# Count blocks of one node per step instead of a pair, in a four-layer graph network

## The chip, the cores and the metric

The kernel runs on one core of one Trainium2 chip, as one launch. The metric is device time in microseconds of a whole execution; less is better. Engines are named as in the profile: PE (TensorE), PEld (its weight load), DVE (VectorE), ACT (ScalarE), POOL (GpSimd), SP (SyncE).

## The reference

6250 nodes have 64 features, and 206250 edges (`src`, `dst`) are sorted by `dst`. Four residual layers follow each other, each followed by a layer norm:

```python
x = _layernorm(x + _L0_gnn_ref(x, edge_attr_32, src, dst, ...))   # mlp: segment_sum(relu([x[src], x[dst], a] @ W1 + b1) @ W2 + b2, dst)
x = _layernorm(x + _L1_gnn_ref(x, edge_index, edge_attr_16, ...)) # gatv2: 4 heads, softmax over each node's edges, batch norm, gelu
x = _layernorm(x + _L2_gnn_ref(x, edge_index, W, a))              # gat: 1 head, softmax over each node's edges, elu
x = _layernorm(x + _L3_gnn_ref(x, src, dst))                      # mean of x[src] over each node's edges
```

The last layer's mean is `segment_sum(x[src], dst) / max(count, 1)`. All inputs are fp32.

## The kernel before

The edges lie in 1612 tiles of 128. Seven tiles make a batch (`B`), and there are 231 batches (`NB`). `prepare` makes tables from the lists of edges. Then `edge_pass` runs three times, as mlp, gatv2 and gat, with `dense` behind each for the work by node, and `mean_layer` comes last. In a trace the tiles of the passes begin with `mlp_`, `gatv_` and `gat_`.

**A batch of an edge pass.** POOL issues one indirect gather of table rows per tile (L469) into a ring of eight batches (`G`, `GQ = 8`). In mlp it waits for `z_made` of six batches back. SP loads the edges' window-relative destination numbers (`rel`), windows of the destination table (`win`) and edge features (`attrT`). DVE compares `rel` to make two one-hot arrays of 7 x 128 columns, `hot` (L487) and `same` (L494, ring of four). PE makes `z` from features and windows (`make_z`, L806 and L810), DVE adds the gathered rows (L508), ACT applies the nonlinearity, PE sums edges that share a destination (`make_sums`, L846), and ACT and SP write them out. mlp has the flag `hist`, under which DVE makes two more one-hots (`count`, L560 and L562) and PE counts the nodes as sources (`add_counts`, L855). Each engine has a `step(i)` in which the order of its work for batch i and its neighbours is written out by hand. `over_batches` runs the first `start` batches unrolled, and the rest in a hardware loop of `U` batches per round.

**Count blocks.** The mean layer gathers nothing. For each step, which is one edge tile together with one destination, there is a column of counts that says how many edges come from every source node. A source is split into a low part (128 values, `src_lo`) and a high part (49 values, `HI`), so a block of a step is a one-hot of 128 times a one-hot of keys. Before, a step holds a pair of nodes: 98 keys (`KEYS`), 4736 steps (`NS`) in 37 columns (`SB`). The steps are found in mlp's unrolled batches. `prepare` spreads tile numbers; SP stores the list `step_of` at batch 7 (L392, one number per element) and loads it back with the tiles' rows (`load_steps`); in batches 14 to 45 PE runs `turn_steps` (L881 to L886) for 37 groups of 128 steps, two a batch, with three copies by ACT each (`copy_cols`, L764); DVE mixes the keys (`step_work`). Then the blocks are built beside the passes: DVE makes one-hots of the next steps (`build_hots`, L635 and L637), PE multiplies them, one matmul of 98 columns per step into a PSUM bank, contiguous (`build_block`, L865), ACT copies groups of five blocks (`copy_block`, L729), and SP stores them to `blocks` in DRAM, once a batch. `BUILD` says which batches build how many: mlp nine a batch from 48, gatv2 five and gat ten a batch from 0, all to 215. Constants that DVE compares with (`iota_of`, `lane_of`, `rel_of`) lie in PSUM (`in_psum`) in bf16.

**The mean layer.** It runs over 74 half blocks of 64 steps (`MEAN_HALVES`). SP loads one (L1965), PE multiplies it by the nodes' features, split into three bf16 parts of 65 columns, with 49 matmuls of 195 columns (L2035), in which the weights are columns of the block with a stride. DVE adds the three parts, PE joins rows of one node (L2010, L2014), and the rest is division, the layer norm, and an indirect load and store by node.

## Time and profile before

| what | value |
|---|---|
| median of three runs | 8260.32 us (8241.33 to 8264.79) |
| span of the profiled execution | 6975.1 us |
| busy in it: PE, PEld, DVE, ACT, POOL | 80%, 70%, 68%, 21%, 71% |
| gathers of mlp, gatv2 and gat | 1612 each |
| iterations of the mean layer | 74 |

The span is the stretch that the profiler shows between the first and the last instruction; the measured time is longer. The stages follow each other with little overlap: `prepare` to 87 us, mlp to 2111, its dense to 2240, gatv2 to 4258, its dense to 4448, gat to about 6496, its dense to about 6600 and the mean layer to the end. PE's clock in the tables is a share of full speed: 1.00 is 2.4 GHz, 0.50 is 1.2 GHz, and values between are mixtures.

### The profile page before, as it was taken

The numbers are of one execution on the slowest core, as the hardware profiler recorded it, in microseconds if no ns is written. First come the engines' busy times: TensorE is split into PE (matmuls) and PEld (weight loads), VectorE is DVE, ScalarE is ACT, GpSimd is POOL, SyncE is SP. The second block draws the span as 40 slices with busy tenths as digits, with TensorE's granted clock in tenths as the row PEclk, the third lists the DMA queues.
The fourth block names the chain that finished last, engine by engine and source line by source line (L and its number), as shares of the span: only waits on it lengthen the run. The fifth ranks groups of instructions, "written<-read, shape, count | busy, mean of one in ns | idle before, by whom it ended". The sixth has DMA issues, their size and how long they took to land. (4 is left out here: it accounts for less than half of the span.)

```text
span 6975.1 us, 134144 instructions
## 1 busy us (share of the span) xinstructions
PE 5545.7 (80%) x36891; PEld 4916.1 (70%) x36891; DVE 4763.3 (68%) x7973; ACT 1449.0 (21%) x4328; POOL 4949.6 (71%) x5209
## 2 busy tenths in 40 slices
PE   5897888777776778888778885588888888888399
PEld 4676777666665666666666663588888888887399
DVE  4557777777755788888888875566666666666455
ACT  1112222222212222222222221222222222222200
POOL 4777777777775777777777776377777777777444
PEclk6556555666665555555555555555555555555599
DMA  6756666666653555555555553554545555554397
GB/s 158 180 144 155 159 159 159 159 158 160 159 149 87 152 146 146 146 145 146 145 146 145 146 146 80 63 112 110 110 110 110 110 110 110 110 110 95 117 360 292
DMA packets 1384856, 995.18 MB, mean 143 GB/s; under 512 B 927331, under 2 KB 1293029, under 8 KB 1375046
## 3 DMA queue, kind: packets, MB, share of 16 engines
q1 hardware_dynamic: 906390, 750.00, 36.6%
q0 software_dynamic: 165856, 169.99, 14.7%
q10 hardware_dynamic: 312400, 72.71, 5.1%
q8 instruction: 92, 1.51, 0.1%
q14 instruction: 118, 0.97, 0.0%
HBM read 676.85 MB, written 315.92 MB: 142 GB/s over the span
## 5 line engine op out<-in xcount | busy, mean ns | idle before, releaser
L469 POOL DMA_INDIRECT gat_G<-gat_src,src_cols x1612 | 1530.2, 949 | 592.8 <-issue 490.3
L469 POOL DMA_INDIRECT mlp_G<-mlp_src,src_cols x1612 | 1533.4, 951 | 533.5 <-issue 487.2
L469 POOL DMA_INDIRECT gatv_G<-gatv_src,src_cols x1612 | 1527.5, 948 | 524.8 <-issue 491.0
L810 PE MATMUL gat_z<-gat_win,gat_hot 128*128 128x1 f32 x3234 | 721.0, 352 | 274.4 <-DVE gat_msg L552 212.9
L810 PEld LDWEIGHTS gat_z<-gat_win,gat_hot 128*128 128x128 f32 x3234 | 707.3, 330 | 318.8 <-issue 279.7
L806 PE MATMUL gatv_z<-attr_w,gatv_attrT 112*128 112x448 f32 x462 | 425.1, 1024 | 408.6 <-DVE gatv_msg L552 398.8
L846 PE MATMUL gat_sums<-gat_msg,gat_same 128*128 128x65 f32 x3234 | 713.6, 410 | 0.0
L846 PEld LDWEIGHTS gat_sums<-gat_msg,gat_same 128*128 128x128 f32 x3234 | 708.2, 330 | 0.0
L846 PE MATMUL gatv_sums<-gatv_msg,gatv_same 128*128 128x68 f32 x3234 | 689.6, 403 | 0.0
L846 PEld LDWEIGHTS gatv_sums<-gatv_msg,gatv_same 128*128 128x128 f32 x3234 | 687.3, 321 | 0.1
L846 PE MATMUL mlp_sums<-mlp_act_out,mlp_same 128*128 128x64 f32 x3234 | 632.7, 374 | 0.0
L846 PEld LDWEIGHTS mlp_sums<-mlp_act_out,mlp_same 128*128 128x128 f32 x3234 | 604.6, 286 | 0.4 <-issue 0.4
L508 DVE TENSOR_TENSOR mlp_zs<-mlp_z,mlp_G 128x448 f32<-128x448 f32 x231 | 144.2, 624 | 642.0 <-DMA mlp_G<-mlp_src,src_cols 612.1
L806 PE MATMUL mlp_z<-attr_w,mlp_attrT 128*128 128x256 f32 (+1 forms) x924 | 482.6, 624 | 79.7 <-DVE mlp_hot L487 47.3
L508 DVE TENSOR_TENSOR gat_z<-gat_z,gat_G 128x7 f32<-128x7 f32 x231 | 40.1, 174 | 637.0 <-DMA gat_G<-gat_src,src_cols 636.8
L810 PEld LDWEIGHTS gatv_z<-gatv_win,gatv_hot 128*128 128x128 bf16 x4851 | 303.7, 134 | 232.3 <-issue 232.3
L806 PEld LDWEIGHTS gatv_z<-attr_w,gatv_attrT 112*128 112x128 f32 x462 | 115.7, 311 | 452.6 <-issue 451.9
L712 ACT ACTIVATE mlp_act_out<-mlp_zs 128x448 f32<-128x448 f32 x231 | 133.2, 577 | 1374.5 <-DVE mlp_zs L508 1283.5
L810 PEld LDWEIGHTS mlp_z<-mlp_win,mlp_hot 128*128 128x128 bf16 x4851 | 335.0, 132 | 115.3 <-issue 91.8
L865 PE MATMUL mlp_build_ps<-mlp_build_area 128*128 128x98 bf16 x1512 | 168.6, 260 | 300.3 <-ACT mlp_build_area L729 300.3
L508 DVE TENSOR_TENSOR gatv_z<-gatv_z,gatv_G 128x448 f32<-128x448 f32 x231 | 146.1, 632 | 365.6 <-DMA gatv_G<-gatv_src,src_cols 365.6
L865 PEld LDWEIGHTS mlp_build_ps<-mlp_build_area 128*128 128x128 bf16 x1512 | 103.3, 121 | 355.8 <-ACT mlp_build_area L729 312.3
(494 smaller groups left out, 10679.4 us busy)
## 6 DMA issues: line engine op xcount, KB each, us to landing
mean_block<-blocks SPq DMA_DIRECT2D x74, 1568.0 KB, 10.1
sums_gatv<-gatv_out_rows SPq DMA_DIRECT2D x231, 252.0 KB
sums_gat<-gat_out_rows SPq DMA_DIRECT2D x231, 231.0 KB, 2.4
blocks<-gat_build_area SPq DMA_DIRECT2D x216, 245.0 KB
mlp_rel<-rel_rows SPq DMA_DIRECT2D x231, 224.0 KB
sums_mlp<-mlp_out_rows SPq DMA_DIRECT2D x231, 224.0 KB
gatv_rel<-rel_rows SPq DMA_DIRECT2D x231, 224.0 KB
gat_rel<-rel_rows SPq DMA_DIRECT2D x231, 224.0 KB
```

The source lines that it names most:

```text
L469: pool.indirect_dma_start(out=G[:, b.gq, j * L.gathered:(j + 1) * L.gathered], out_offset=None, in_=L.gather_table, in_offset=bass.Indirec ...
L508: nc.vector.tensor_tensor(total.rearrange("p (b w) -> p b w", w=w), made.rearrange("p (b w) -> p b w", w=w), Gv[:, b.gq, :, L.gathered - w ...
L712: act.activation(act_out[:, b.q, :], zs[:, b.q, :], ACT.Relu).then_inc(act_done, 1)
L806: pe.matmul(z[b.q % 2][:, t0 * w:(t0 + nt) * w], attrT[0:nt * ax, b.q, g, :], S["attr_w"][ax][0:nt * ax, 0:nt * w], start=True, stop=True)
L810: last = pe.matmul(z[b.q % 2][:, j * w:(j + 1) * w], hot[:, b.q, j, :], win[:, b.q, j, part * w:(part + 1) * w], start=not ax and part == ...
L846: last = pe.matmul(sums[b.q % 2][:, j * L.msg:(j + 1) * L.msg], same[:, b.q, j, :], rhs, start=True, stop=True)
L865: last = pe.matmul(build_in[g % len(build_in)][:, j * KEYS:(j + 1) * KEYS], hot_src[:, b.c % 2, k + j, :], hot_key[:, b.c % 2, k + j, :], ...
```

## The change

A step holds one node. There are 7936 steps in 62 columns, with 49 keys each. Eight steps make an octet, which is the unit in which DVE, PE and ACT work, with two PSUM rings replaced by one bank that ACT has to empty before the next octet. mlp builds four octets a batch in batches 48 to 199, gatv2 two a batch in 8 to 199, gat none. ACT copies an octet into a half (128 steps, 1.6 MB) in SBUF, in the space of `masks` or `work`, and SP stores a half when it is full. In the one-hots of blocks and counts two steps lie innermost, so that every operand of the comparison has two packed bf16 elements there; `hot` of mlp and gatv2 is compared with a pattern of 32 packed lanes. PE therefore reads those one-hots with a stride of two elements, and writes a step's block to every eighth element of PSUM. Two-slot `same` in mlp, an `act_out` that shares the place of `zs` in mlp, and other sharing of memory make room. The steps are found in five portions at batches 8 to 55, with four groups a batch; the key mixing has two operations per portion instead of four; `U` is 16, and `start` is 24 in gatv2. The mean layer runs 62 iterations of 128 steps over contiguous weights, with five slots for blocks, and its setup of rows has fewer operations. The dense stages read the longer `step_of`. The diff, cut to its core:

```diff
-U = 8
+U = 16
...
-PAIRS = N // 2
-NS = ETILES + PAIRS - 1
-SB = NS // P
-assert SB * P == NS and NS // P + 1 <= 2 * D
-KEYS = 2 * HI
-STEP_ROWS = 40 * P
-NONE = 200.0
-GROUP = 5
+SB = -(-(ETILES + N - 1) // P)
+NS = SB * P
+STEP_ROWS = 64 * P
+assert SB <= D and NS <= STEP_ROWS and N + NTP <= STEP_ROWS
+FAR_KEY = 64.0
 PASS_C = 216
-BUILD = {"mlp": (48, PASS_C, 9, 0), "gatv2": (0, PASS_C, 5, 1512), "gat": (0, PASS_C, 10, 2592)}
-NSP = 2592 + PASS_C * 10
+K2, OCTET = 2, 8
+HALF_OCTETS = P // OCTET
+HALF_W = HI * P
+BUILD = {"mlp": (48, 200, 4, 0), "gatv2": (8, 200, 2, 608), "gat": (0, 0, 0, 992)}
 assert all(BUILD[a][3] + (BUILD[a][1] - BUILD[a][0]) * BUILD[a][2] == BUILD[b][3]
-           for a, b in (("mlp", "gatv2"), ("gatv2", "gat"))) and NSP >= NS
+           for a, b in (("mlp", "gatv2"), ("gatv2", "gat"))) and BUILD["gat"][3] * OCTET == NS
 ROW_W = 4 * P
-THIRD = -(-SB // 3)
-THIRDS = [(0, THIRD), (THIRD, THIRD - 1), (2 * THIRD - 1, THIRD - 1)]
-assert THIRDS[-1][0] + THIRDS[-1][1] == SB
-LOAD_AT, HOT_AT, GROUPS_AT, KEYS_AT = (8, 22, 34), (11, 25, 37), (14, 27, 39), (22, 34, 46)
-LOADS = 4
+PORTION = -(-SB // 5)
+PORTIONS = [(0, PORTION), (PORTION, PORTION)] + [(2 * PORTION + k * (PORTION - 1), PORTION - 1) for k in range(3)]
+assert PORTIONS[-1][0] + PORTIONS[-1][1] == SB
+LOAD_AT, HOT_AT, GROUPS_AT, KEYS_AT = (tuple(a + 8 * h for h in range(5)) for a in (8, 10, 11, 15))
+LOADS, GROUPS_EACH = 7, 4
...
-        same = sb("same", [P, Q, B, P])
+        SQ = Q if soft else 2
+        same = sb("same", [P, SQ, B, P])
         out_rows = sb("out_rows", [P, Q, B * L.row])
...
+        rel_of, lane_of, lanes_of = (consts[:, o:o + w] for o, w in ((0, NT), (LANES, 1), (LANES, D // 2)))
+        steps2_of = consts[:, STEPS2:CONSTS].rearrange("p (e k) -> p e k", k=K2)
...
-            hot_hi = sb("hot_hi", [P, 2, B, HI], BF16)
-            hot_lo = sb("hot_lo", [P, 2, B, P], BF16)
+            hot_hi = sb("hot_hi", [P, 2, OCTET // K2, HI, K2], BF16)
+            hot_lo = sb("hot_lo", [P, 2, OCTET // K2, P, K2], BF16)
...
+        build_from, build_end, per_batch, first_octet = BUILD[L.name]
+        block_count = (build_end - build_from) * per_batch
+        build_ps = pb("build_ps", [P, 512])
+        build_of = build_ps[:, 0:OCTET * HI].rearrange("p (h e) -> p h e", e=OCTET)
+        if per_batch:
+            ring = 2 * per_batch
+            hots = sb("hots", [P, max(ring * OCTET * (P + HI), PORTION * ROW_W if hist else 0)], BF16)
+            hot_src = hots[:, 0:ring * OCTET * P].rearrange("p (q g e k) -> p q g e k", q=ring, g=OCTET // K2, k=K2)
+            hot_key = hots[:, ring * OCTET * P:ring * OCTET * (P + HI)].rearrange(
+                "p (q g e k) -> p q g e k", q=ring, g=OCTET // K2, k=K2)
+            area = hots[:, :].bitcast(F32)
+        else:
+            area = sb("area", [P, TA])
+        if hist:
+            step_rows = hots[:, 0:PORTION * ROW_W].rearrange("p (b w) -> p b w", w=ROW_W)
...
-                o = i + (-2)
+                o = i + (-3)
                 if o.exists() and builds(o):
-                    wait(sp, blocks_copied, built(o))
-                    sp.dma_start(S["blocks"][:, bass.ds(first_of(o) * KEYS, per_batch * KEYS)],
-                                 block_out[:, o.c % 2, :]).then_inc(blocks_out[o.c % 2], 16)
+                    k, loops = half_of(o, per_batch)
+                    if k % HALF_OCTETS == 0:
+                        h = k // HALF_OCTETS - 1
+                        wait(sp, blocks_copied, octet(o, per_batch))
+                        sp.dma_start(S["blocks"][:, bass.ds((loops + (h + first_octet // HALF_OCTETS)) * HALF_W, HALF_W)],
+                                     halves[h % 2].rearrange("p h e -> p (h e)")).then_inc(blocks_out[h % 2], 16)
                 if hist and isinstance(i.n, int) and i.n == 1:
                     sp.wait_ge(S["steps_spread"], 16 * RB)
                     sp.dma_start(step_in[:, :], S["step_tile"][0:NS, :].rearrange("(b e) o -> b (e o)", e=P)
...
-                nc.vector.tensor_tensor(hot[:, b.q, :, :], relv[:, b.q, :, :],
-                                        bc(lane_of, 2, [P, B, P]), ALU.is_equal).then_inc(hot_made, 1)
+                if L.win_dt == BF16:
+                    nc.vector.tensor_tensor(
+                        hot[:, b.q, :, :].rearrange("p b (a e) -> p (b a) e", e=D // 2),
+                        rel[:, b.q, :].rearrange("p (b e) -> p b e", e=D // 2), bc(lanes_of, 1, [P, 4 * B, D // 2]),
+                        ALU.is_equal
+                    ).then_inc(hot_made, 1)
+                else:
+                    nc.vector.tensor_tensor(hot[:, b.q, :, :], relv[:, b.q, :, :],
+                                            bc(lane_of, 2, [P, B, P]), ALU.is_equal).then_inc(hot_made, 1)
 
...
-                wait(dve, sums_made, b.used(Q))
-                nc.vector.tensor_tensor(same[:, b.q, :, :], relv[:, b.q, :, :],
+                wait(dve, sums_made, b.used(SQ))
+                nc.vector.tensor_tensor(same[:, b.c % SQ, :, :], relv[:, b.q, :, :],
...
-            def build_hots(b):
-                wait(dve, blocks_made, built(b, back=2))
-                cols = bass.ds(first_of(b), per_batch)
-                nc.vector.tensor_tensor(hot_src[:, b.c % 2, :, :], bc(iota_of, 1, [P, per_batch, P]),
-                                        bc(S["src_lo"][:, cols], 2, [P, per_batch, P]), ALU.is_equal)
-                nc.vector.tensor_tensor(hot_key[:, b.c % 2, :, :], bc(iota_of[:, 0:KEYS], 1, [P, per_batch, KEYS]),
-                                        bc(S["keys"][:, cols], 2, [P, per_batch, KEYS]), ALU.is_equal
-                                        ).then_inc(hots_made, 1)
+            def build_hots(b, k):
+                if hist and isinstance(b.n, int) and b.n == build_from:
+                    dve.wait_ge(groups_made, SB)
+                wait(dve, blocks_made, octet(b, k + 1 - ring))
+                cols = bass.ds((octet(b, k) + first_octet) * OCTET, OCTET)
+                for hot_of, of_step, w in ((hot_src, S["src_lo"], P), (hot_key, S["keys"], HI)):
+                    last = nc.vector.tensor_tensor(
+                        hot_of[:, slot(b, k), :, :, :], bc(steps2_of[:, 0:w, :], 1, [P, OCTET // K2, w, K2]),
+                        bc(of_step[:, cols].rearrange("p (g k) -> p g k", k=K2), 2, [P, OCTET // K2, w, K2]), ALU.is_equal)
+                last.then_inc(hots_made, 1)
...
-                        chain(v.tensor_scalar(rho_h, rho_h, -1.0, 2.0, ALU.max, ALU.min))
-                        chain(v.scalar_tensor_tensor(out=mixed_h, in0=rho_h, scalar=1.0, in1=rho_h,
-                                                     op0=ALU.subtract, op1=ALU.mult))
-                    if n == KEYS_AT[h] + 1:
-                        chain(v.scalar_tensor_tensor(out=mixed_h, in0=mixed_h, scalar=2.0, in1=rho_h,
-                                                     op0=ALU.mult, op1=ALU.add))
-                        chain(v.scalar_tensor_tensor(out=keys_h, in0=mixed_h, scalar=float(HI), in1=keys_h,
-                                                     op0=ALU.mult, op1=ALU.add))
+                        chain(v.tensor_scalar(mixed_h, rho_h, 0.0, FAR_KEY, ALU.not_equal, ALU.mult))
+                        v.tensor_tensor(keys_h, mixed_h, keys_h, ALU.add).then_inc(keys_made, 1)
...
-            def copy_block(b, g):
-                k, m = build_groups[g]
-                wait(act, blocks_made, built(b, g + 1))
-                if g == 0:
-                    wait(act, blocks_out[b.c % 2], (b.loop * (U // 2) + (b.c - build_from) // 2) * 16)
-                act.activation(block_out[:, b.c % 2, k * KEYS:(k + m) * KEYS],
-                               build_in[g % len(build_in)][:, 0:m * KEYS], ACT.Copy
-                               ).then_inc(blocks_copied, 1)
+            def copy_octet(b, k):
+                wait(act, blocks_made, octet(b, k + 1))
+                at, loops = half_of(b, k)
+                h, e = at // HALF_OCTETS, at % HALF_OCTETS * OCTET
+                if e == 0:
+                    if hist and isinstance(b.n, int):
+                        wait(act, keys_made, len(PORTIONS))
+                    if h >= 2:
+                        wait(act, blocks_out[h % 2], (loops // 2 + h // 2) * 16)
+                act.activation(halves[h % 2][:, :, e:e + OCTET], build_of, ACT.Copy).then_inc(blocks_copied, 1)
 
             def copy_tails(n):
...
-            def build_block(b, g):
-                k, m = build_groups[g]
-                wait(pe, hots_made, built(b) // len(build_groups) if isinstance(b.n, int)
-                     else b.n + (1 - build_from))
-                wait(pe, blocks_copied, built(b, g + 1) - len(build_in))
-                for j in range(m):
-                    last = pe.matmul(build_in[g % len(build_in)][:, j * KEYS:(j + 1) * KEYS], hot_src[:, b.c % 2, k + j, :],
-                                     hot_key[:, b.c % 2, k + j, :], start=True, stop=True)
+            def build_octet(b, k):
+                if hist and isinstance(b.n, int) and b.n == build_from and k == 0:
+                    pe.wait_ge(cols_copied, 3 * SB)
+                wait(pe, hots_made, octet(b, k + 1))
+                wait(pe, blocks_copied, octet(b, k))
+                for e in range(OCTET):
+                    g, j = e // K2, e % K2
+                    last = pe.matmul(build_of[:, :, e], hot_src[:, slot(b, k), g, :, j], hot_key[:, slot(b, k), g, :, j],
+                                     start=True, stop=True)
                 last.then_inc(blocks_made, 1)
 
...
-                    build_block(p, 0)
+                    build_octet(p, 0)
                 if L.window and (i + 1).exists():
                     make_z(i + 1)
+                if p.exists() and builds(p) and per_batch == 4:
+                    build_octet(p, 1)
...
+                if p.exists() and builds(p) and per_batch == 4:
+                    build_octet(p, 2)
                 if hist and p.exists():
                     add_counts(p)
                 if hist and isinstance(i.n, int) and i.n < start:
                     turn_steps(i.n)
-                if p.exists() and builds(p) and len(build_groups) > 1:
-                    build_block(p, 1)
+                if p.exists() and builds(p):
+                    build_octet(p, per_batch - 1)
                 if isinstance(i.n, int) and i.n >= turns_at:
...
-            for c, (s, n) in enumerate(MEAN_HALVES):
-                j, k = c // 2, c % 2 * MSTEPS
-                pe.wait_ge(block_in[2 * (j % SLOTS) + c % 2], 16 * (j // SLOTS + 1))
+            for c in range(H):
+                pe.wait_ge(block_in[c % SLOTS], 16 * (c // SLOTS + 1))
                 wait(pe, parts_added, c - 1)
-                w = rows_of(c)
-                counts = block[:, j % SLOTS, k * KEYS:(k + n) * KEYS].rearrange("p (e h) -> p h e", h=HI)
+                counts = block[:, c % SLOTS, :, :]
                 for h in range(KN):
...
-                    last = pe.matmul(y[c % 2][0:w, 0:3 * W], counts[:, h, :], parts[:, h, :], start=h == 0,
+                    last = pe.matmul(y[c % 2][:, 0:3 * W], counts[:, h, :], parts[:, h, :], start=h == 0,
                                      stop=h == KN - 1)
```

## Rows read from the trace of the kernel before

**Rows 1.** The page, part 1: busy time of each engine.

```profile
PE 5545.7 (80%) x36891; PEld 4916.1 (70%) x36891; DVE 4763.3 (68%) x7973; ACT 1449.0 (21%) x4328; POOL 4949.6 (71%) x5209
```

**Rows 2.** Table by stretch: length, busy (count), clock, DMA share, GB/s.

```profile
87.00:520.00 433.00, 363.15 (x2480) 309.60 (x2479) 215.79 (x268) 69.72 (x203) 329.30 (x340) 0.56 0.70 168
...
560.00:1900.00 1340.00, 1076.37 (x8426) 930.66 (x8425) 962.13 (x1072) 303.39 (x612) 1012.87 (x1074) 0.61 0.62 159
...
2600.00:3500.00 900.00, 722.15 (x4634) 583.99 (x4634) 723.69 (x1236) 192.32 (x618) 680.24 (x721) 0.52 0.56 146
...
4448.00:5400.00 952.00, 815.54 (x4377) 790.36 (x4375) 646.44 (x1070) 203.41 (x741) 715.03 (x758) 0.50 0.51 110
...
6624.00:6961.00 337.00, 337.00 (x3826) 337.00 (x3823) 182.07 (x859) 32.96 (x213) 138.52 (x140) 1.00 0.87 340
```

**Rows 3.** Gathers by line: busy, mean ns, then idle and what ended it.

```profile
L469 POOL DMA_INDIRECT mlp_G<-mlp_src,src_cols x1612 | 1533.4, 951 | 533.5 <-issue 487.2 <-POOLq L954 42.4 <-PE mlp_z L810 4.0
...
L469 POOL DMA_INDIRECT gatv_G<-gatv_src,src_cols x1612 | 1527.5, 948 | 524.8 <-issue 491.0 <-POOLq L2187 32.5 <-PE gatv_z L810 1.3
```

**Rows 4.** Waits in 87 to 560 us: total us, times, longest.

```profile
PE mlp_z L806 <- DMA mlp_win<-mlp_dst: 26.6, 4, 18.5
...
POOL mlp_G L469 <- PE mlp_z L810: 0.3, 1, 0.3
```

**Rows 5.** PE's timeline in the mean layer, and its block loads (page, part 6).

```profile
6624.73 4.42 PE L2035 MATMUL mean_y<-mean_parts,mean_block 128*128 128x195 bf16 x49
...
6629.40 4.42 PE L2035 MATMUL mean_y<-mean_parts,mean_block 128*128 128x195 bf16 x49
...
mean_block<-blocks SPq DMA_DIRECT2D x74, 1568.0 KB, 10.1
```

**Rows 6.** PE's timeline, mlp batch without groups: start, us, line, operation.

```profile
406.10 0.94 PE L855 MATMUL mlp_count_ps<-mlp_hot_lo,mlp_hot_hi 128*49 128x128 bf16 x7
...
407.99 0.85 PE L810 MATMUL mlp_z<-mlp_win,mlp_hot 128*128 128x64 bf16 x12
...
409.43 0.69 PE L810 MATMUL mlp_z<-mlp_win,mlp_hot 128*128 128x64 bf16 x9
...
413.08 0.94 PE L855 MATMUL mlp_count_ps<-mlp_hot_lo,mlp_hot_hi 128*49 128x128 bf16 x7
```

**Rows 7.** PE's timeline, mlp batch with two groups of steps.

```profile
256.70 0.94 PE L855 MATMUL mlp_count_ps<-mlp_hot_lo,mlp_hot_hi 128*49 128x128 bf16 x7
257.58 0.29 PE L881 MATMUL mlp_build_ps<-masks,mlp_step_rows 128*128 128x128 bf16 x1
...
260.13 0.26 PE L881 MATMUL mlp_build_ps<-masks,mlp_step_rows 128*128 128x128 bf16 x1 [0.80 <-ACT masks L764]
...
267.90 0.94 PE L855 MATMUL mlp_count_ps<-mlp_hot_lo,mlp_hot_hi 128*49 128x128 bf16 x7
```

**Rows 8.** PE's timeline, block matmuls in a batch of mlp.

```profile
1402.62 0.51 PE L865 MATMUL mlp_build_ps<-mlp_build_area 128*128 128x98 bf16 x4
1405.19 0.59 PE L865 MATMUL mlp_build_ps<-mlp_build_area 128*128 128x98 bf16 x5 [2.07 <-ACT mlp_build_area L729]
```

**Rows 9.** Copies of four blocks by ACT in mlp, by form.

```profile
L729 ACT ACTIVATE mlp_build_area<-mlp_build_ps 128x392 bf16<-128x392 f32 x168 | 82.2, 489 | 2.9 <-PE mlp_build_ps L865 2.6
```

**Rows 10.** DVE's comparisons and one one-source operation, by form.

```profile
L635 DVE TENSOR_TENSOR gat_build_area<-gat_in_psum,src_lo 128x1280 bf16<-128x1280 bf16 x216 | 318.1, 1473 | 0.0
...
L487 DVE TENSOR_TENSOR mlp_hot<-mlp_rel,mlp_in_psum 128x896 bf16<-128x896 bf16 x231 | 248.8, 1077 | 26.9 <-DMA mlp_rel<-rel_rows 26.7
...
L508 DVE TENSOR_TENSOR mlp_zs<-mlp_z,mlp_G 128x448 f32<-128x448 f32 x231 | 144.2, 624 | 642.0 <-DMA mlp_G<-mlp_src,src_cols 612.1 <-issue 26.5 <-PE mlp_z L810 3.3
...
L637 DVE TENSOR_TENSOR gatv_build_area<-gatv_in_psum,keys 128x490 bf16<-128x490 bf16 x216 | 141.9, 657 | 0.0
...
L1178 DVE TENSOR_SCALAR masks<-masks 128x3328 f32<-128x3328 f32 x1 | 1.9, 1894 | 0.0
```

## What the change was predicted to do, and why

> **What bounds the kernel now.** I read the busy shares first [rows 1]: PE 80%, POOL 71%, DVE 68%, none at its end, so the kernel has stages with different limits. The profiled execution spans 6975.1 us, while the median of the timed runs is 8260.32; the 1285.2 us between them lie outside the span. I take them as unchanged, so the sum is made in microseconds of the span and put on the median. Next the table by stretch [rows 2]: in the three edge passes (mlp, gatv2, gat) PE is busy about 80 to 86% at a granted clock of 0.50 to 0.61, and in the last stretch, the mean layer, PE is busy 337.0 of 337.0 us at clock 1.00. Then the gather line [rows 3]: each pass issues 1612 indirect gathers; in gatv2 they take 1527.5 us plus 491.0 us of issue, 1.25 us each, so 8.74 us for a batch of seven. 231 batches are 2019 us. mlp gives (1533.4 + 487.2)/231 = 8.75 us, and gat has a row of the same kind. Hardly anything else ends POOL's idle time: all three passes last as long as POOL needs to issue gathers, and PE and DVE hide below it. The mean layer, in contrast, is bound by PE.
>
> POOL can be stopped in one way: before batch n's gathers it waits until PE has made z of batch n-6. So PE may be about six batches late, 6 x 8.74 = 52 us, less the few microseconds between z and the end of its batch: I estimate 49. In the stretch from 87 to 560 us POOL waited for PE once, 0.3 us [rows 4]: the cushion is just spent there and no more.
>
> **The part that gains: the mean layer.** The steady iteration is 4.675 us: its 49 matmuls begin at 6624.73 and 6629.40 [rows 5], and so on to the end. It reads one 1568 KB block with 10.1 us to landing. Before there are 74 iterations of 64 steps of node pairs; after there are 62 of 128 one-node steps, with the same 49 matmuls 195 columns wide: 12 x 4.675 = -56.1 us. A block is 1605 KB after, one per 4.675 us, the same rate as now (340 GB/s at a DMA share of 0.87 [rows 2]), and five blocks in flight cover a 10.1 us landing. The weights become contiguous; 4.42 us for 49 matmuls is modelled with its end, and the start-to-start pace is (4.675 - 0.40)/49 = 87 ns where 195 columns at 2.4 GHz are 81. If stride causes the difference it is worth 49 x 6 ns x 62 = -18; if not, nothing; the two small matmul groups between are more likely part of it. I take -5, range -10 to 0. The setup loses about eight small DVE operations at 0.2 to 0.3 us: -2, as part of them lies beside DMA. The steps' table that the dense stage before it broadcasts grows from 4736 to 7936 entries, and a few [P,1] operations are added in prepare: +2 (0 to 4). Net -61.
>
> **The part that costs: making the steps, in mlp's first batches.** Each group of 128 steps needs four bf16 matmuls, four tiny ones and three copies by ACT. A batch with no group takes PE 6.99 us, from its counts at 406.10 to the next at 413.08 [rows 6], and that at 1.2 GHz with PE full. A batch with two groups takes 267.90 - 256.70 = 11.20 us, and the first group is 260.13 - 257.58 = 2.55 us, of which 0.80 is a wait for ACT's copies [rows 7]; the second, followed by z, is 11.20 - 6.99 - 2.55 = 1.66. There are 62 groups instead of 37, and four in a batch instead of two: 6.99 + 3 x 2.55 + 1.66 = 16.3 us, against 8.74 that POOL offers. Over batches 11 to 46 that is 15 batches of 16.3, two of two or one group (about 8.7 to 11.2), and 19 light ones of 6.99: some 393 us of PE against 36 x 8.74 = 315 of POOL. PE ends 78 us late; it also starts some 13 us late (an 18.5 us wait for the window load [rows 4]) and perhaps 5 to 8 us more, as 7936 single elements are stored instead of 4736 on SP's queue ahead of the loads (before: 6.4 us for an issue queued behind them). So 78 + 13 against a cushion of 49 leaves a stall of about 42 us. Some 9 us of this kernel's long gathers in that stretch would overlap it: +33, range 0 to 60. DVE's key mixing is smaller than before (2 operations for 4), and hidden. Nothing behind this stretch gives back a POOL stall, because POOL is the bound from there on.
>
> **The blocks in mlp, batches 48 to 199.** Before: nine matmuls of 98 columns a batch and two copies, 48 to 215. After: four octets, that is 32 matmuls of 49 columns in four bursts, each copied by ACT before the next may begin. A batch of PE: the present pace at 1.2 GHz is 81 ns for 98 columns [rows 8] and 53 for 64 (0.85 us for 12 against 0.69 for 9 [rows 6]), so 49 columns are 41 to 53 ns, an octet 0.33 to 0.42 us, say 0.45 with its wait. Hand-offs: between octets 2 and 3 only the counts (0.94 us) lie, and between octet 3 and the next octet 0 nothing; ACT's copy of 392 columns is 0.49 us [rows 9] plus signals, so about 0.85 us of waits a batch. 6.99 + 1.8 + 0.85 = 9.64 us at 1.2 GHz, about 5.7 at 2.4. It fits in 8.74 as soon as 15% of the time is at 2.4 GHz (0.907 x 0.85 + 1.533 x 0.15 = 1.0); before, the clock column is 0.61 in 560 to 1900 [rows 2], that is 22%. So 0, range to +150 (see the rivals). The present batch shows a 2.07 us wait of PE for ACT [rows 8] and the pass still went by POOL: that wait is slack.
>
> DVE there: at present all its two-source operations cost 1.025 ns per element per partition plus 161 ns: 1280 elements 1473 ns, 896 1077, 490 657 [rows 10], fp32 or bf16 alike. An octet's one-hots have 1024 + 392 elements: 1.21 + 0.56 = 1.77 us at that rate. If the two packed bf16 innermost halve the slope, 0.69 + 0.36 = 1.05. A batch then has hot 0.62, same 1.08, z+G 0.62, the counts' one-hots 1.05, four octets 4.2: about 7.6 us, under 8.74. I take this one: these operations now read one source broadcast along the innermost dimension, after the change no operand does. That this chip has a doubled rate shows in a one-source fp32 operation: 3328 elements in 1894 ns, 0.57 ns each [rows 10]. At the full rate see the third rival.
>
> The Trainium skill is split on this. "VectorE: DVE Perf Modes", § The perf-mode tier table, gives tensor_tensor 1x with any PSUM operand, and the steps' pattern lies in PSUM; its § Why PSUM operands drop a tier allows the 16-bit double mode there, and "Vector Engine (DVE) Microarchitecture Reference", § 5.1, asks only for 2-byte types, step one and more than one innermost element. No row of before shows the case; by the first the third rival comes about.
>
> `same` in two slots instead of four waits for sums two batches back, which PE made already when DVE comes to it: 0. Blocks stored as 1.6 MB per four batches instead of 220 KB each: DMA share is 0.61 to 0.62 in mlp, and the total falls from 119 to 99.5 MB: 0.
>
> **gatv2 and gat.** gatv2: two octets in place of five matmuls, DVE less than before; gat loses its blocks. Both are POOL-bound with slack (PE 0.80 and 0.86 busy at clock 0.5), so nothing comes of it: 0. That is where most of the removed work lies, and it buys nothing.
>
> **Sum.** -56.1 - 5 - 2 + 2 + 33 = -28.1: 8260.3 - 28 = 8232, rounded 8232. A measurement of this kernel can tell about 0.3%, 25 us, from no change, so the forecast lies on that edge.
>
> **Rivals.**
> (a) The steps cost no stall: the clock rises to 2.4 GHz while PE is full, or the start lag is smaller. For it: PE catches up at twice the pace whenever the clock is granted, and it is 0.56 mean in 87 to 520 [rows 2]; against it: in the full stretch of rows 6 it stays at the slow pace. Then -61: 8199.
> (b) PE becomes the bound in the block stage: octet hand-offs or PSUM writes 32 bytes apart cost more than 0.9 us a batch over my figure or the clock stays at 0.5. One mechanism, decided at 8.74 us of PE a batch. At 9.64 it is 152 x 0.9 = +137; with the -28 it is 8370, slower. For it: 9.64 exceeds 8.74 already; against: clock 0.61 with less PE work. No row shows a strided PSUM write; by the rows a matmul is bound by its columns. "PSUM — Partial Sum Buffer", § Specifications (TRN2), says that any non-contiguous access slows matmuls significantly; by that this rival is the likely one, and no run here shows it yet.
> (c) DVE stays at the full rate: 0.62 + 1.08 + 1.08 + 1.77 + 4 x 1.77 = 11.6 us a batch against 8.74: 2.85 x 152 = +433; in gatv2 DVE is busy 723.69 of 900 us [rows 2], 7.03 us a batch, less 1.47 plus 3.54 is 9.1 against 8.74: 0.36 x 192 = +69. With the -28: 8734.
> (d) The 1285 us outside depend on the kernel (for instance on the count of gathers, which is unchanged): no row speaks for a change.
>
> **Chances.** Forecast 0.48 (8232, of its own range 8195 to 8260: 0.28 faster, 0.16 same, 0.04 slower), (a) 0.22, faster, (b) 0.18, of which 0.03 same and 0.15 slower, (c) 0.12, slower. Faster 0.50, same 0.19, slower 0.31. The range has to take in (a) and (b) with the bounds of their costs and leaves out (c) and the ends: 8175 to 8440.
>
> **What would show it.** After: the mean loop 62 iterations at 4.6 to 4.675 us; POOL's gather idle in mlp with a new releaser, PE's z, near 40 us between batches 15 and 50, and PE's batch with four groups 16 us; in batches 48 to 199 the gather pace stays 8.74 us and DVE's 1024-element one-hots take 0.69 us (1.21 would mean (c)); PE's octet of eight 0.33 to 0.42 us at 1.2 GHz (over 0.6 would mean (b)); gatv2 and gat as long as now. I am wrong if the gather pace in mlp's build stage exceeds 8.8 us, or if mlp's stall lies far from 33.

## The result and the profile after

The changed kernel takes 8920.23 us (median of four, 8906.11 to 8932.43). The kernel before, measured with it, takes 8256.37. The ratio is 1.080, with a 95% interval of 1.078 to 1.082: 8% slower, where 8232 and a small gain were forecast.

The numbers can't be read without one fact: the measurements, each of which ran on another chip, are of two kinds. On three chips the kernel before took 6982, 6985 and 6994 us, and the rows ahead of the prediction come from such an execution; on three others it took 8244, 8246 and 8270, on a fourth 8456, and the result above is of their kind. I call them quick and slow chips. The page of the changed kernel is of a slow one: its span is 8930.7 us and its time 8932.43. 1.7 us lie outside the span, where I had taken 1285.2 from the span and the median. First the page's busy time by engine (columns as in [rows 1]), then the gathers by line (columns as in [rows 3]), both of the changed kernel:

```profile
PE 5740.3 (64%) x39642; PEld 5033.8 (56%) x39642; DVE 4188.2 (47%) x8609; ACT 1423.0 (16%) x4375; POOL 4914.5 (55%) x5185
...
L494 POOL DMA_INDIRECT mlp_G<-mlp_src,src_cols x1612 | 1526.9, 947 | 1649.5 <-PE mlp_z L843 1080.4 <-issue 424.2 <-remote 103.5
L494 POOL DMA_INDIRECT gatv_G<-gatv_src,src_cols x1612 | 1526.6, 947 | 1059.4 <-issue 422.0 <-PE gatv_z L843 408.2 <-remote 155.3
L494 POOL DMA_INDIRECT gat_G<-gat_src,src_cols x1612 | 1528.7, 948 | 928.7 <-issue 423.7 <-remote 398.0 <-POOLq L2192 97.5
```

A gather takes 947 ns, as before. What is new is the wait for PE's z in mlp, 1080.4 us, and in gatv2, 408.2, where [rows 3] had 4.0 and 1.3. POOL no longer bounds mlp.

To see what belongs to the change and what to the chip, both kernels were profiled on one slow chip (b0_see and a0_pair below). Stages run from the first gather of a pass to that of the next, and then to the end of the span, in us; the quick columns are the execution of [rows 1] and a_u8 (below):

| stage | before, slow | changed, slow | difference | before, quick | changed with loops of 8, quick | difference | forecast |
|---|---|---|---|---|---|---|---|
| mlp and its dense | 2606.3 | 3320.5 | +714 | 2152.4 | 2326.8 | +174 | +33 |
| gatv2 and its dense | 2629.6 | 2692.3 | +63 | 2208.3 | 2271.8 | +64 | 0 |
| gat and its dense | 2548.2 | 2502.4 | -46 | 2159.9 | 2162.7 | +3 | 0 |
| mean | 367.8 | 305.9 | -62 | 367.2 | 307.3 | -60 | -61 |

The table by stretch of the block stage (columns as in [rows 2]), first before and then changed, on that slow chip:

```profile
590.00:1850.00 1260.00, 942.94 (x6637) 796.17 (x6636) 758.50 (x833) 250.35 (x494) 796.79 (x842) 0.57 0.55 132
```

```profile
640.00:2960.00 2320.00, 1305.56 (x12185) 1148.08 (x12185) 1088.89 (x2007) 448.51 (x951) 1055.82 (x1118) 0.65 0.41 108
```

PE is busy 75% in the first and 56% in the second: the engine with more to do waits more. From the start of batch 56 to that of batch 199 the gathers follow each other at 10.45 us a batch before and at 14.7 after. (The two stretches as a whole give about 10.5 and 14.5: 842 and 1118 instructions of POOL, seven a batch; the second begins ahead of the block stage.)

### The profile page after: what moved, and what is told of

Its sections match the earlier page's. It is cut to its first block and busy times, and to the rows that moved or that the text cites. A ratio compares the mean times of both kernels' runs of the same rounds, so it can differ in the third digit from the quotient of the medians.

```text
span 8930.7 us, 138161 instructions
## 1 busy us (share of the span) xinstructions
PE 5740.3 (64%) x39642; PEld 5033.8 (56%) x39642; DVE 4188.2 (47%) x8609; ACT 1423.0 (16%) x4375; POOL 4914.5 (55%) x5185
## 5 line engine op out<-in xcount | busy, mean ns | idle before, releaser
L494 POOL DMA_INDIRECT mlp_G<-mlp_src,src_cols x1612 | 1526.9, 947 | 1649.5 <-PE mlp_z L843 1080.4
L900 PE MATMUL mlp_build_ps<-mlp_hots 128*128 128x49 bf16 x4864 | 434.9, 267 | 986.8 <-ACT masks L759 347.7
L900 PEld LDWEIGHTS mlp_build_ps<-mlp_hots 128*128 128x128 bf16 x4864 | 356.5, 138 | 1034.8 <-issue 720.6
L577 DVE TENSOR_TENSOR gat_diff<-gat_act_out,gat_z 128x7 f32<-128x7 f32 x231 | 37.4, 162 | 1359.0 <-DMA mlp_d_into<-carry_mlp 1349.1
L900 PE MATMUL gatv_build_ps<-gatv_hots 128*128 128x49 bf16 x3072 | 310.9, 288 | 489.6 <-issue 466.0
L879 PE MATMUL mlp_sums<-mlp_zs,mlp_same 128*128 128x64 f32 x3234 | 591.0, 354 | 43.9 <-issue 43.6
L879 PEld LDWEIGHTS mlp_sums<-mlp_zs,mlp_same 128*128 128x128 f32 x3234 | 565.9, 268 | 47.8 <-issue 47.3
L900 PEld LDWEIGHTS gatv_build_ps<-gatv_hots 128*128 128x128 bf16 x3072 | 272.7, 154 | 524.7 <-issue 523.3
L584 DVE TENSOR_TENSOR gatv_msg<-gatv_G,gatv_z 128x448 f32<-128x448 f32 x231 | 143.3, 620 | 728.4 <-issue 504.6
L526 DVE TENSOR_TENSOR mlp_same<-mlp_rel,mlp_in_psum 128x896 f32<-128x896 bf16 x231 | 250.7, 1085 | 436.5 <-PE mlp_sums L879 236.3
L593 DVE TENSOR_TENSOR mlp_hot_hi<-mlp_in_psum,hilo 128x392 bf16<-128x392 bf16 x231 | 105.9, 459 | 730.1 <-remote 627.1
```

The costliest lines, as they stand in the source:

```text
L494: pool.indirect_dma_start(out=G[:, b.gq, j * L.gathered:(j + 1) * L.gathered], out_offset=None, in_=L.gather_table, in_offset=bass.Indirec ...
L526: nc.vector.tensor_tensor(same[:, b.c % SQ, :, :], relv[:, b.q, :, :], bc(rel_of[:, bass.ds(b.n * B, B)], 2, [P, B, P]), ALU.is_equal).the ...
L577: nc.vector.tensor_tensor(diff[:, b.q, :], logits[:, b.q, :], max_in[(b.q + 1) % 2][:, 0:B * H], ALU.subtract).then_inc(diff_ready, 1)
L584: nc.vector.tensor_tensor(msg[:, b.q, :, 0:D].rearrange("p b (h c) -> p b h c", c=c), Gv[:, b.gq, :, 0:D].rearrange("p b (h c) -> p b h c" ...
L593: last = nc.vector.tensor_tensor(hot_of[:, b.c % 2, :, :, :], bc(steps2_of[:, 0:w, :], 1, [P, OCTET // K2, w, K2]), bc(cols[:, bass.ds(b.n ...
L879: last = pe.matmul(sums[b.q % 2][:, j * L.msg:(j + 1) * L.msg], same[:, b.c % SQ, j, :], rhs, start=True, stop=True)
```

## Why a slow chip is slow, and where the kernel before has its 1285 us

**b0_see** is the kernel before, unchanged.

> The kernel before, for its profile. On a chip where it takes 8260: 10.2 to 10.6 us a batch in every pass, with the signal of PE's last z of a batch 4 to 6 us behind the end of its matmul instead of at it. Elsewhere as in its first profile, 8.74 us a batch.

It took 8240.04 us with a span of 8238.0, and the passes show the difference: 10.45, 10.60 and 10.46 us a batch against 8.74. Of the 1263 us between the two spans 454, 421 and 388 lie in mlp, gatv2 and gat with the dense stage behind each (the first has 31 of them in its dense), and 0.5 in the mean layer. In the line of the gathers:

```profile
L469 POOL DMA_INDIRECT gat_G<-gat_src,src_cols x1612 | 1529.6, 949 | 976.1 <-issue 422.2 <-PE gat_z L810 333.3 <-remote 123.8
```

Duration and issue are as ever, but there are waits for PE's z of 333.3 us and others of 123.8 us that the profile can't assign ("remote"). So nearly all of the 1285 us lies in the passes, 1.7 to 1.9 us a batch. A caution on releasers: the traces of slow chips hold a fifth of the records of semaphore updates (46267 in b0_see, 216860 for the same kernel in the execution of [rows 1]), so a name behind an arrow can be wrong there, as it is at L577 below, and only the starts are safe. The timeline tells how. In gat of the changed kernel on a slow chip:

```profile
7004.81 3.12 PE L843 MATMUL gat_z<-gat_win,gat_hot 128*128 128x1 f32 x14 [3.33 <-DVE gat_msg L584]
...
7007.86 0.59 PE L854 MATMUL gat_z<-ident,hilo 7*128 7x8 f32 x2
...
7011.16 0.94 POOL L494 DMA_INDIRECT gat_G<-gat_src,src_cols  x1 [0.30 <-issue]
...
7013.70 0.16 DVE L577 TENSOR_TENSOR gat_diff<-gat_act_out,gat_z 128x7 f32<-128x7 f32 x1 [6.21 <-DMA mlp_d_into<-carry_mlp]
...
7013.89 0.94 POOL L494 DMA_INDIRECT gat_G<-gat_src,src_cols  x1 [1.78 <-remote]
```

DVE's subtraction (L577) waits for PE's turned maximum (L854), which is made at 7008.45 (7007.86 + 0.59), and begins at 7013.70, 5.2 us later, when the last gather (issued until 7012.10) has had time to land. POOL's next gather begins with it. On a quick chip, with the same code:

```profile
5205.01 0.59 PE L856 MATMUL gat_z<-ident,hilo 7*128 7x8 f32 x2
...
5205.64 0.16 DVE L579 TENSOR_TENSOR gat_diff<-gat_act_out,gat_z 128x7 f32<-128x7 f32 x1 [1.00 <-PE gat_z L856]
```

L579 begins at 5205.64, 0.04 us behind the end of L856's matmuls (5205.01 + 0.59). So on a slow chip a signal of PE can come some us late while gathers are under way, and each stretch from PE to another engine and back costs more.

These rows are no exception. In gat of the changed kernel, over batches 10 to 224, L577 begins 5.2 us behind the end of L854 in the median and 0.36 to 0.44 us behind the last packet of the batch's last gather (the middle half); in a_u8 it begins 0.04 us behind the matmuls, wherever the packets are. In mlp of the changed kernel I take the copies of octets for which ACT stood idle. Where the octet ended with a gather under way (from its start on POOL to its last packet; 452 copies), the copy began 1.62 us later in the median, and over 1 us later in 52% of them; where none was under way (155 copies), 0.04 us later, and never over 1 us. (In a_best, below, it is over 1 us in 63% of 390 copies against 13% of 205.) Two rows of one batch show the second case, with POOL idle from 2403.24 to 2409.45:

```profile
2405.46 0.81 PE L900 MATMUL mlp_build_ps<-mlp_hots 128*128 128x49 bf16 x8 [4.97 <-ACT work L759]
...
2406.39 0.50 ACT L759 ACTIVATE masks<-mlp_build_ps 128x392 bf16<-128x392 f32 x1 [0.61 <-PE mlp_build_ps L900]
```

Signals of ACT and DVE are prompt in the same trace with gathers under way: from ACT's copy to PE's next octet 0.14 us, from ACT's exponentials to DVE's messages 0.03, from DVE to PE's z in gat 0.08, as in a_u8. So what comes late is PE's signals, and nearly always beside gathers. That the gathers are the cause is still read from times alone: no run took them away on a slow chip, as the one meant for it (a_load, below) fell on quick chips twice. No chip is on record twice, so that the chip makes the difference, and not the hour or the kernels measured beside it, is likely but not shown either. The unedited changed kernel was always beside a slow kernel before; the expectation of a_best_fast asked for this, and without the changed kernel there the kernel before took 8456 us, near neither 6984 nor 8260.

Two more runs belong here. **b0_base** and **b0_timed** are the kernel before again.

> The kernel before, unchanged, profiled beside the others. Its earlier profile spans 6975 us while its timed runs take 8260; the profile of the changed kernel spans 8931 and its runs take 8920. Theory A (the earlier profile caught an execution that the timed ones are not like): span near 8260, and POOL's batch of seven gathers takes about 10.3 us instead of 8.74, as in the changed kernel, (8260 - 6975)/693 = 1.85 us more a batch. Theory B (1285 us lie outside the span for good): span again 6975 and 8.74 us a batch.

> The kernel before, unchanged, for its profile on a chip on which it takes 8260 us, if this is one. Theory late signals (on such a chip what PE signals while POOL's gathers are under way arrives only when the batch's last gather has landed, 1.5 to 1.8 us after POOL has issued it): every pass at 10.2 to 10.6 us a batch against 8.74, 3 x 231 x 1.6 = 1110 us and more in mlp's first batches, which makes the 1285 us; the mean layer as before, 4.675 us an iteration. Theory outside (1285 us lie ahead of or behind the program): passes at 8.74. On the other kind of chip: 6975 to 6995 us and 8.74 us.

Both fell on quick chips: 6994.78 and 6983.61 us (b0_timed against the kernel before 1.000, 0.999 to 1.001), 8.74 to 8.76 us a batch, so neither showed where the 1285 us are. What they showed is that the quick execution of the rows ahead of the prediction is no product of the profiler: the eight timed runs of b0_timed had it too. b0_see came after them and found the other kind.

## Is it the longer loop?

**b_u16**: the kernel before with

```diff
-U = 8
+U = 16
```

> The kernel before with loops of 16 batches a round instead of 8, nothing else. Theory code (a round of the loop no longer stays with the engine and is fetched anew each round, as the instruction queues of the changed kernel show: 9.9 MB against 2.5): instruction traffic rises to 8 MB or more, engines show idle stretches of 1 to 7 us that nothing releases, and the time rises by 300 to 700 us towards 8900. Theory work (the octets' hand-offs on PE and ACT are what costs): unchanged within 30 us of the kernel before.

6991.0 us against 6982.2 for the kernel before and 6994.78 for the same kernel as b0_base, all on one chip: no cost that shows. The code is indeed fetched anew in the loops (page, part 3, before and b_u16: packets and MB of the two queues of instructions):

```profile
q8 instruction: 92, 1.51, 0.1%
q14 instruction: 118, 0.97, 0.0%
```

```profile
q8 instruction: 200, 3.28, 0.2%
q14 instruction: 467, 3.82, 0.2%
```

7.1 MB instead of 2.5, and hidden. **a_u8**: the changed kernel with loops of 8 in two passes:

```diff
+    global U
+    U = {"mlp": 8, "gatv2": 16, "gat": 8}[L.name]
-    loops = (NB - start) // U - 1
+    loops = (200 - start) // U
```

> The changed kernel with rounds of 8 batches in mlp and gat and 16 only in gatv2. Theory code: mlp falls from 3134 us by several hundred, to 14.65 less at least 3 us a batch in its block stage, gat falls little (its waits are 1.5 us a batch), gatv2 stays at 2511 us. Theory work: mlp stays at 14.6 us a batch in batches 56 to 199.

It fell on a quick chip: 7157.64 us against 6982.2 for the kernel before, ratio 1.025. The longer loop is not needed to explain it, as this kernel has loops of 8 in mlp. The block stage takes 9.65 us a batch, the groups' stage 48 us more than POOL's pace where the kernel before has 10 to 13. The changed kernel itself was meant to follow on such a chip:

> The changed kernel as it is, in three rounds beside the kernel before. On this chip the kernel before took 6982 us and its profile is the one of the forecast; the pair measured first took 8256 and 8920. Theory chip (that measurement fell on a chip on which PE's signals come late, and the change suffers more there): here 7150 to 7250, ratio 1.025 to 1.04, as the same kernel with loops of 8 in mlp and gat took 7158. Theory same everywhere: ratio 1.08 here too, 7540.

**a0_again**, **a0_pair** and **a0_look** all fell on slow chips: 8917.07, 8912.07 and 8906.03 us, with ratios of 1.079, 1.080 and 1.079. So its time on a quick chip was not measured, and that of a_u8 stands for it. I take the 3% there and the 8% here for one loss under two lengths of signal. What loops of 16 add to the changed kernel was not measured by itself: on a slow chip a_dve (below), with loops of 8 in mlp and gat, came within 5 us of it, but on quick chips a_load (loops of 16) takes 10.1 us a batch in the block stage and a_u8 (loops of 8) 9.65, and nothing here says whether the loops or the plain loads make that difference.

## What holds up the block stage

Waits of a_u8 in 760 to 2000 us (who waited for whom: us in total, times, longest), and the line of the octets there (busy, mean ns, then PE's idle time ahead of them):

```profile
DVE mlp_same L528 <- PE mlp_sums L881: 261.2, 127, 3.2
PEld mlp_build_ps L902 <- DVE mlp_hots L672: 192.8, 77, 4.8
PE mlp_build_ps L902 <- ACT masks L761: 159.6, 100, 4.6
POOL mlp_G L496 <- PE mlp_z L845: 152.0, 76, 2.9
PE mlp_build_ps L902 <- ACT work L761: 110.5, 85, 3.5
...
L902 PE MATMUL mlp_build_ps<-mlp_hots 128*128 128x49 bf16 x4047 | 339.9, 257 | 292.1 <-ACT masks L761 159.6 <-ACT work L761 110.5 <-DVE mlp_hots L672 20.1
```

and the table by stretch of its block stage:

```profile
560.00:2010.00 1450.00, 1111.18 (x11542) 988.56 (x11542) 1021.64 (x1907) 427.24 (x905) 991.26 (x1051) 0.72 0.59 159
```

PE is busy 1111 of 1450 us, at a clock of 0.72, that is 44% of the time at 2.4 GHz, and a batch still takes 9.65 us. So it isn't PE's work alone that bounds it. PE idles 292.1 us ahead of its octets in 1240 us, 2.3 us a batch, and 270 us of that end with a copy by ACT: the circle PE, ACT, PE. (The 192.8 us of the weight load for DVE's one-hots are hidden behind it except for 20.1.) In the rows of a_u8 an octet's copy follows at once; on a slow chip it doesn't:

```profile
1405.32 0.84 PE L902 MATMUL mlp_build_ps<-mlp_hots 128*128 128x49 bf16 x8
...
1406.19 0.50 ACT L761 ACTIVATE masks<-mlp_build_ps 128x392 bf16<-128x392 f32 x1 [2.62 <-PE mlp_build_ps L902]
```

```profile
2411.52 0.51 PE L900 MATMUL mlp_build_ps<-mlp_hots 128*128 128x49 bf16 x8
...
2415.14 0.50 ACT L759 ACTIVATE masks<-mlp_build_ps 128x392 bf16<-128x392 f32 x1 [4.78 <-remote]
2415.78 0.51 PE L900 MATMUL mlp_build_ps<-mlp_hots 128*128 128x49 bf16 x8 [3.24 <-issue]
```

PE's octet ends at 1406.16 and ACT copies at 1406.19; in the second rows it ends at 2412.03, ACT copies at 2415.14, and only then does PE make the next octet. There are four hand-offs a batch, of which those that end beside gathers come late. I tried three edits of a_u8, all on one slow chip beside a0_again (8917, loops of 16); a_u8 itself was not measured there, so each difference from 8917 holds the shorter loops too, and each edit was run once. **a_pe** spreads the octets and puts two copies ahead of the nonlinearity, which waits for gathered rows:

```diff
@@ ACT's order
+                early = 2 if per_batch == 4 else 0
+                if p.exists() and builds(p):
+                    for k in range(early):
+                        copy_octet(p, k)
                 if L.window and i.exists():
                     nonlinear(i)
@@ PE's order, between the two groups of z and behind them
-                    make_z(i + 1)
-                if p.exists() and builds(p) and per_batch == 4:
-                    build_octet(p, 1)
+                    make_z(i + 1, (lambda: build_octet(p, 1)) if spread else None)
+                if spread:
+                    build_octet(p, 2)
@@ PE, behind the sums and ahead of the counts
-                if p.exists() and builds(p) and per_batch == 4:
-                    build_octet(p, 2)
+                if spread:
+                    build_octet(p, 3)
```

> The kernel with loops of 8, and in mlp octet 1 lies between the two halves of z, octet 2 behind z, octet 3 ahead of the counts, and ACT copies octets 0 and 1 before its nonlinearity. Theory hand-off (PE waits for ACT's copies of neighbouring octets and for copies queued behind the gather): PE's waits for the copies (270 us in 760 to 2000) fall below 60, and the block stage from 9.65 to 8.75 to 9.0 us a batch, 90 to 130 us in all. Theory ring (DVE waits for sums before it makes same): little, under 30 us.

8756.47 us: 161 less, and the block stage at 13.6 us a batch instead of 14.7. Whether PE's waits for the copies fell below 60 us can't be read from a slow chip's trace. **a_dve** changes DVE's order in mlp, so that its wait for PE's sums stands behind the one-hots of the blocks:

```diff
-                if i.exists():
+                if i.exists() and not hist:
                     same_destination(i)
...
                     for k in range(per_batch):
                         build_hots(i, k)
+                if i.exists() and hist:
+                    same_destination(i)
```

> The kernel with loops of 8, and in mlp DVE makes same behind the one-hots of counts and octets, so that its wait for sums two batches back (261 us in 760 to 2000, ring of two) no longer stands ahead of them. Theory ring: PE's waits for octet one-hots (213 us there) vanish and the block stage falls to about 8.75 to 9.2 us a batch, 60 to 130 us. Theory hand-off: under 30 us.

8922.47 us, the block stage at 14.6: on a slow chip the wait for the ring of two costs nothing by itself, and neither do loops of 16, unless the one hides the other. **a_psum** writes contiguous columns:

```diff
-        build_of = build_ps[:, 0:OCTET * HI].rearrange("p (h e) -> p h e", e=OCTET)
+        build_of = build_ps[:, 0:OCTET * HI].rearrange("p (e h) -> p h e", e=OCTET)
```

> The kernel with loops of 8 (7158 us), and PE writes each step's block to contiguous PSUM columns, while ACT reads with a stride. There an octet takes 0.59 to 0.62 us from its start to the next work at 1.2 GHz, 74 to 78 ns for 49 columns, where the forecast had 41 to 53. Theory stride: the octet falls to 0.33 to 0.45 us, a batch of the block stage from 9.65 to about 9.0 us, the time by 80 to 110 us. Theory other (weights read with a stride, or signals): octet and time unchanged within 15 us; a slower copy by ACT (over 0.50 us) would add.

```profile
2408.42 0.49 PE L902 MATMUL mlp_build_ps<-mlp_hots 128*128 128x49 bf16 x8 [5.30 <-ACT masks L761]
2408.78 1.19 PE L841 MATMUL mlp_z<-attr_w,mlp_attrT 128*128 128x256 f32 x2
```

From the octet to z it is now 0.36 us, 45 ns a matmul of 49 columns, against 0.59 to 0.62 (1405.32 to the sums at 1405.94 in a_u8): PSUM writes 32 bytes apart cost some 30 ns a matmul, and ACT's copy, now with the stride on its read, still takes 0.50 us. In the Trainium skill, "PSUM — Partial Sum Buffer", § Specifications (TRN2), says that non-contiguous access slows matmuls, and this trace agrees. But the time fell by 20 us only (8897.43 against 8917.07): between the two profiled executions (8903.25 and 8897.43) mlp and its dense lost 37 us, with the block stage at 14.4 instead of 14.7, but gatv2 and its dense took 29 more, for which I have no cause. So the matmuls are little of what the stage waits for there; what the stride costs by itself on a quick chip was not measured. Then all three together, **a_all**:

> The changed kernel with loops of 8 in mlp and gat, octets spread between z's halves, sums and counts, ACT's copies ahead of its nonlinearity, contiguous PSUM columns, and DVE's same behind the one-hots. On the chip of 8260 the spread order alone gave 8756 and contiguous columns 22 us: about 8715. On the chip of 6982: the block stage from 9.65 to 8.75 us a batch, 7158 - 131 = about 7030; still above the kernel before, as mlp's group stage (48 us) and gatv2 (57 us) stay, less 60 in the mean layer.

On a quick chip, 7012.26 us against 6984.65. mlp's block stage is at 8.74 us a batch, POOL's pace: the 131 us that a_u8 had lost there are back, with as many octets. PE's idle time ahead of them fell from 2.3 to 1.1 us a batch (163.4 us in 600 to 1850). Which of the three edits does it on a quick chip is not separated; on the slow one it was the order. What is left of its loss is 52 us in the groups (10 before) and 0.25 us a batch in gatv2, 176 x 0.25 = 44, against 60 from the mean layer: 42 + 44 - 60 = 26, where 27.6 were measured. **a_222** leaves the orders and deals the octets out anew:

```diff
-BUILD = {"mlp": (48, 200, 4, 0), "gatv2": (8, 200, 2, 608), "gat": (0, 0, 0, 992)}
+BUILD = {"mlp": (48, 200, 2, 0), "gatv2": (8, 200, 2, 304), "gat": (48, 200, 2, 688)}
```

> The changed kernel with two octets a batch in all three passes (304, 384, 304) in place of four, two and none: the same work, half the hand-offs a batch in mlp, moved to gat. Theory hand-off: on the chip of 8260, mlp's block stage falls from 14.7 to about 11 us a batch, gat rises from 10.24 to about 11: 8917 - 3.7 x 144 + 0.75 x 144 = about 8490. On the chip of 6982: mlp's block stage at 8.75 (PE 6.99 + 2 x 0.6 + 0.4), total 7155 - 131 = about 7025 or less. Theory work (matmuls' time counts, wherever they are): total unchanged within 60 us.

7083.58 us on the same quick chip: mlp's block stage at 8.74, as expected, but gat now takes 9.03 us a batch in 8 to 199, 55 us that I had not expected. Half the hand-offs a batch thus bring mlp's block stage to POOL's pace with the old order, the stride and loops of 16 all left as they are. No run gave the octets a second bank, as the kernel before has for its blocks. **a_load** replaces mlp's gathers by plain loads (what it leaves out stands in its text):

```diff
+                    if hist:
+                        r = t % (NP // P) * P
+                        pool.dma_start(out=G[:, b.gq, j * L.gathered:(j + 1) * L.gathered],
+                                       in_=L.gather_table[r:r + P, :]).then_inc(gathered[b.gq], 16)
+                        continue
                     pool.indirect_dma_start(
```

> The changed kernel, with mlp's 1612 indirect gathers replaced by plain loads of 128 neighbouring rows from the same queue's engine (it leaves out the gather by index, so mlp's values differ). On the chip of 8260, theory late signals: without gathers PE's signals come at once, mlp's block stage falls from 14.7 us a batch to PE's own 9.6 to 9.7, the batches without blocks to about 7 us. Theory chip (PE's signals are late there whatever POOL does): it stays at 13 to 15 us. On the chip of 6982: 9.6 us a batch, as PE bounds it there already (9.65).

7168.88 us, and 7185.36 in its repetition (**a_load_slow**), both on quick chips. PE makes 10.1 us a batch in the block stage (9.6 was expected) although nothing gathers by index: there POOL is not what bounds the changed kernel.

## gatv2 and the groups

In gatv2 of a_all:

```profile
3000.80 0.54 PE L910 MATMUL gatv_build_ps<-gatv_hots 128*128 128x49 bf16 x8
...
3001.37 0.50 ACT L763 ACTIVATE masks<-gatv_build_ps 128x392 bf16<-128x392 f32 x1 [6.66 <-PE gatv_build_ps L910]
...
3001.96 0.20 ACT L752 ACTIVATE gatv_z<-gatv_diff 128x28 f32<-128x28 f32 x1
...
3002.19 0.62 DVE L586 TENSOR_TENSOR gatv_msg<-gatv_G,gatv_z 128x448 f32<-128x448 f32 x1 [1.80 <-ACT gatv_z L752]
...
3003.05 1.85 PE L849 MATMUL gatv_z<-attr_w,gatv_attrT 112*128 112x448 f32 x2 [0.55 <-DVE gatv_msg L586]
```

PE's second octet (L910) ends a batch, ACT copies it (L763, 0.50 us) and only then makes its exponentials (to 3002.16, L752), for which DVE's messages (L586) and then PE's z wait. The octet and its copy lie on the circle of the softmax passes, some 1.2 us a batch: the next batch's octet follows 8.78 us later (3000.80 to 3009.58) where POOL needs 8.74, and in the mean of 24 to 199 a batch takes 8.99 us. gat in a_222 has the same order. **a_best** is a_all and takes both off: in gatv2 ACT's copy stands behind its exponentials and nonlinearity, and PE's octet 0 behind the turned logits; in mlp a batch's groups stand behind z, behind the sums and behind the counts, not in a row:

```diff
@@ ACT's order
-                if d.exists() and builds(d):
+                if d.exists() and builds(d) and not soft:
                     copy_octet(d, per_batch - 1)
...
+                if d.exists() and builds(d) and soft:
+                    copy_octet(d, per_batch - 1)
@@ PE's order
-                if p.exists() and builds(p):
+                if p.exists() and builds(p) and not soft:
                     build_octet(p, 0)
...
                     turn_logits(i)
+                if soft and p.exists() and builds(p):
+                    build_octet(p, 0)
...
+                    turn_steps(i.n, slice(0, 1))
...
+                    turn_steps(i.n, slice(1, 2))
...
-                    turn_steps(i.n)
+                    turn_steps(i.n, slice(2, None))
```

> The spread variant (7012 us where the kernel before takes 6984), and on top: in gatv2 ACT's exponentials stand ahead of its copy of the last octet and PE makes octet 0 behind the turned logits; in mlp the groups of steps of a batch lie behind z, behind the sums and behind the counts, so that ACT's copies (0.80 us of wait each) are hidden. If hand-offs are the cause of what is left: gatv2 loses its 43 us, the group stage 15 to 30 of its 52: 6940 to 6955, 0.4 to 0.6% faster than the kernel before. If they are not: 7005 to 7015. Where the kernel before takes 8260: about 8600, as gatv2's and mlp's waits shrink but PE's late signals stay.

On a slow chip 8556.97 us (ratio to the kernel before 1.037, 1.036 to 1.039), where the changed kernel beside it took 8912.07 (1.080, 1.078 to 1.082). About 8600 was expected. gatv2 is back at the kernel before's 10.60 us a batch in 24 to 199; mlp's groups lost 6 us and its block stage is at 12.97. So 355 of 668 us come back with all the work still done: by its order, for the most part, as contiguous columns with loops of 8 gave 20 alone. Most of the other 313 us lies in mlp's block stage, 2.5 us a batch over the kernel before. In its repetitions it took 8569.85 (**a_best_look**, the kernel before 8245.87) and on the chip of 8456 8690.28 (**a_best_fast**, 1.027, 1.020 to 1.034). It was not seen on a quick chip, so what its last two edits are worth there isn't known. No version beat the kernel before.

## Why the prediction was wrong, point by point

- **Outside the span.** "The 1285.2 us between them lie outside the span. I take them as unchanged" failed first. They are in the passes: the sum was made against an execution unlike the timed ones. That alone does not explain the miss, which is there on a quick chip too (+175 us for a_u8, where -28 was forecast). A span far from the median should have been a rival with a price, not a constant; my rival (d) named it and gave it no chance.
- **The block stage at 0.** The term 9.64 us a batch was worked out, and 9.65 was measured on a quick chip, but that agreement is luck: 9.64 was for 1.2 GHz throughout, and with 44% of the time at 2.4 GHz the prediction's own formula gives 8.74 / (0.907 x 0.56 + 1.533 x 0.44) = 7.4. What failed is the step to 0, "it fits in 8.74 as soon as 15% of the time is at 2.4 GHz": 44% was at 2.4 GHz. The mis-sized terms are the hand-offs, 0.85 us a batch, where PE idles 339 us in 150 batches of a_u8, 2.3 us, and the octet, 0.33 to 0.42 us of matmuls, where it takes 0.62. ACT's copy takes 0.50 us at either clock of PE. Worth +131 there, and +615 on a slow chip, where those beside gathers take some us each. "That wait is slack" was right of the kernel before, which makes its blocks in two groups.
- **Rival (b)** is what happened, with 8370 and 0.18; its price was that of a quick chip, and its cause only half right. The stride in PSUM is real (+0.24 us an octet), but worth 20 us on a slow chip; the greater part is the circle and not the matmul.
- **The groups at +33.** +38 on a quick chip (48 against 10): right, and PE's batch with four groups takes 15.3 us in a_u8 (256.59 to 271.85, count to count; 16.3 forecast), with the clock rising in it. On a slow chip +72. That their waits for ACT are the cost is not shown: taking them apart gave 6 us.
- **`same` in two slots at 0.** The reason given, that the sums are made already when DVE comes to them, is wrong: DVE waits 261.2 us for them in a_u8. On a slow chip the wait costs nothing that shows (a_dve).
- **gatv2 at 0.** +64 and +63: I looked at PE's and DVE's busy shares and not at what ACT's copy stands ahead of.
- **gat at 0.** Right on a quick chip (+3). On a slow one gat gained 46 us; its blocks are gone there, and no run takes that alone.
- **DVE at half the slope.** Right: 1024 elements 679 ns (0.69 forecast), 392 elements 349 (0.36), `hot` 609 (0.62).

```profile
L670 DVE TENSOR_TENSOR mlp_hots<-mlp_in_psum,src_lo 128x1024 bf16<-128x1024 bf16 x608 | 412.6, 679 | 5.3 <-remote 4.5
...
L670 DVE TENSOR_TENSOR mlp_hots<-mlp_in_psum,keys 128x392 bf16<-128x392 bf16 x608 | 212.2, 349 | 0.0
L513 DVE TENSOR_TENSOR mlp_hot<-mlp_rel,mlp_in_psum 128x896 bf16<-128x896 bf16 x231 | 140.6, 609 | 56.6 <-DMA mlp_rel<-rel_rows 29.8 <-issue 26.7
```

In all of these rows the pattern (of steps or of lanes) lies in PSUM, and the rate is doubled. In the Trainium skill, "VectorE: DVE Perf Modes", § The perf-mode tier table, gives tensor_tensor 1x with any PSUM operand, and these rows contradict it; "Vector Engine (DVE) Microarchitecture Reference", § 5.1, agrees with them, though it also finds that alignment to four bytes makes no difference, which the next rows may speak against. One exception I had not foreseen is the counts' one-hots (L593, rows of the timeline):

```profile
2403.89 1.21 DVE L593 TENSOR_TENSOR mlp_hot_lo<-mlp_in_psum,hilo 128x1024 bf16<-128x1024 bf16 x1
2419.79 0.68 DVE L593 TENSOR_TENSOR mlp_hot_lo<-mlp_in_psum,hilo 128x1024 bf16<-128x1024 bf16 x1
2433.21 1.21 DVE L593 TENSOR_TENSOR mlp_hot_lo<-mlp_in_psum,hilo 128x1024 bf16<-128x1024 bf16 x1
```

They go 1.21, 0.68, 1.21, 0.68 us from batch to batch, without exception in all 231, 943 ns in the mean. The operation is that of L670, but its columns begin at entry 7 x n of the batch: every second batch begins off a pair of bf16 and gets the single rate, where an octet's columns always begin at a multiple of 8. That the odd start does it is argued from the alternation, and no run changes it. The one-hots' two slots alternate in the same way, but the slots of L670 do too, and its 608 operations all take 0.68 to 0.69 us. The slower rate costs some 0.36 us a batch (0.26 and 0.10), hidden in DVE's slack.

- **The mean layer at -61.** -60 to -62: right, nearly all of it the twelve iterations. Contiguous weights gave 0.02 us an iteration (4.66 against 4.675), 1.2 us and not 5:

```profile
8699.92 4.40 PE L2063 MATMUL mean_y<-mean_parts,mean_block 128*128 128x195 bf16 x49
...
8704.58 4.40 PE L2063 MATMUL mean_y<-mean_parts,mean_block 128*128 128x195 bf16 x49
```

## What to carry to other kernels

Cost an edit by its round trips between engines, not by its busy time alone: here PE, which takes its work in order, waited for ACT's copy of its one buffer and paid 2.3 us a batch, and a copy placed ahead of the exponentials in ACT's queue put itself on the path. Where a profiled execution and the timed runs differ by more than their scatter, find where before adding anything to either; a batch's pace in the loops shows it. A doubled vector rate or a stride is worth what the stage's bound makes of it, here nothing that shows, and 20 us.

## What the runs showed of the hardware

- Two kinds of chip for one kernel: 6982 to 6994 and 8244 to 8270 us (8456 once), with the mean layer alike and durations within 2% for 119 of 136 groups of instructions (most of the rest are PE's, whose clock varies). What differs is when PE's signals arrive while gathers are under way: 0.04 us behind the modelled end of the matmul, or in gat of the changed kernel 5.2 in the median. With no gather under way they are prompt on a slow chip too (0.04 in the median of mlp's copies), and so are those of ACT and DVE beside gathers (0.03 to 0.14). Why is open; so is whether they wait for the gathers. A slow execution is known by its pace, and its trace by having a fifth of the records of semaphore updates.
- Loops of 16 batches have more of their code fetched again (7.1 MB in all against 2.5), which cost the kernel before nothing that shows (6991.0 us beside 6982.2 and 6994.78).
- One-hots of 1024 bf16 elements take 679 ns with the pair packed innermost and its start even, 1210 when the start is odd (argued), with one source in PSUM in both.
- A matmul of 49 bf16 columns from 128 rows takes 45 ns into contiguous PSUM (a_psum) and 74 to 78 ns with columns 32 bytes apart (a_u8), at a granted clock of 0.5, as eighths of an octet. Medians from start to start of neighbouring matmuls are 42 and 81 ns at 0.5, and 27 and 43 ns at 1.0.
